# A fused attention and fp8 layer: the quantisation and bias of a head, in two halves, one behind each unit

## The reference

```python
xn = _layernorm(x)
# attention: 16 heads of 16 features over all 4096 tokens, softmax in float32
scores = einsum('bhqd,bhkd->bhqk', q, k);  ctx = einsum('bhqk,bhkd->bhqd', softmax(scores), v)
attn = ctx @ out_w.T + out_b
# ffn: both operands rounded to fp8 (e4m3), one scale for all of a tensor
x_fp8 = clip(xn * scale, -448, 448).astype(float8_e4m3fn)
ffn = (x_fp8 @ w_fp8.T * (x_scale * w_scale) + bias).astype(bfloat16)
```

## Time and profile before

| | us |
|---|---|
| median of three runs | 1858.34 (1856.72 to 1859.45) |
| the profiled execution | 1859.34 |
| its span, first to last instruction | 1857.5 |
| ACT busy | 1732.1 (93%) |
| PE busy | 1639.1 (88%) |
| DVE busy | 1606.8 (87%) |
| mean granted TensorE clock | 0.995 |

### The profile page before, as it was taken

How to read it: one execution, slowest core, us unless ns; L and a number is a source line. 1 busy time by engine, 2 the same in 40 slices (tenths; PEclk the granted TensorE clock), 3 DMA queues, 4 the chain that set the end, 5 groups by cost and what they waited for, 6 DMA issues and landing times.

```text
span 1857.5 us, 74891 instructions
## 1 busy us (share of the span) xinstructions
PE 1639.1 (88%) x33482; PEld 563.5 (30%) x33482; DVE 1606.8 (87%) x1831; ACT 1732.1 (93%) x1898; POOL 44.9 (2%) x57
## 2 busy tenths in 40 slices
PE   6889998998998889999988888888888888888888
PEld 4522322222222222222322222222222222222226
DVE  8689989899898989989888898888898988888895
ACT  2299999999999999999999999999999999999990
POOL 0000000000000000000000000000000000000003
PEclk9999999999999999999999999999999999999999
DMA  6401111101111111011110101101010001001014
GB/s 200 146 23 41 36 33 43 30 20 30 41 35 34 43 31 30 19 42 36 35 33 19 35 12 30 24 20 29 22 32 13 14 19 24 19 16 27 16 35 135
DMA packets 130169, 70.62 MB, mean 38 GB/s; under 512 B 79216, under 2 KB 120432, under 8 KB 129840
## 3 DMA queue, kind: packets, MB, share of 16 engines
q1 hardware_dynamic: 127920, 64.38, 13.1%
q10 hardware_dynamic: 1920, 1.39, 0.3%
HBM read 43.39 MB, written 17.83 MB: 33 GB/s over the span
## 4 chain that ended last, share of the span: by engine, by line
ACT 43%; issue 26%; PE 17%; DVE 10%; SPq 1%; DMA 1%; POOL 1%; ACTq 0%; DVEq 0%; POOLq 0%
ACT probs L851 43%; PE banks L1559 8%; PE banks L1505 5%; DVE bits L1203 2%; PE banks L1527 2%; DVE d_probs L1221 1%; DVE horner L1210 1%; DVE horner L1216 1%; DVE powers L1213 1%; PE banks L1409 1%; PE banks L1399 1%; DVE ctx_out L1181 1%; DVE powers L1207 1%; DVE o_sb L1180 1%; SPq L561 1%
## 5 line engine op out<-in xcount | busy, mean ns | idle before, releaser
L851 ACT ACTIVATE probs<-banks 128x1024 f32<-128x1024 f32 x1856 | 1709.1, 1140 | 18.4 <-issue 12.5
L1559 PE MATMUL banks<-probs,v_st 64*32 64x512 f32 x14848 | 970.1, 590 | 1.9 <-DVEq L1185 1.1
L1505 PE MATMUL banks<-q_st,k_st 50*32 50x512 f16 x16384 | 772.5, 381 | 185.2 <-ACT probs L851 166.6
L1505 PEld LDWEIGHTS banks<-q_st,k_st 50*32 50x32 f16 x16384 | 230.3, 89 | 1099.5 <-ACT probs L851 949.6
L1203 DVE TENSOR_SCALAR bits<-banks 128x1024 int32<-128x1024 f32 x192 | 235.0, 1224 | 86.9 <-PE banks L1505 81.6
L1559 PEld LDWEIGHTS banks<-probs,v_st 64*32 64x32 f32 x14848 | 264.9, 106 | 62.1 <-DVEq L1185 6.4
L1213 DVE SCALAR_TENSOR_TENSOR powers<-powers,horner 128x1024 f32<-128x1024 int32 x192 | 235.7, 1227 | 6.6
L1210 DVE SCALAR_TENSOR_TENSOR horner<-powers 128x1024 f32<-128x1024 int32 x192 | 235.5, 1227 | 6.6
L1216 DVE SCALAR_TENSOR_TENSOR horner<-powers,horner 128x1024 f32<-128x1024 f32 x192 | 235.2, 1225 | 6.6
L1221 DVE SCALAR_TENSOR_TENSOR d_probs<-horner,bits 128x1024 int32<-128x1024 f32 x192 | 235.1, 1225 | 6.6
L1207 DVE TENSOR_SCALAR powers<-bits 128x1024 int32<-128x1024 int32 x192 | 133.2, 694 | 6.6
(11 more groups left out here) (105 smaller groups left out, 426.5 us busy)
## 6 DMA issues: line engine op xcount, KB each, us to landing
late_x<-xnT_copy SPq DMA_DIRECT2D x32, 256.0 KB, 3.2
k_st<-k_parts SPq DMA_DIRECT2D x102, 64.0 KB, 2.3
q_st<-q_parts SPq DMA_DIRECT2D x198, 32.0 KB, 1.9
k_st<-k_parts SPq DMA_DIRECT2D x102, 60.0 KB, 2.2
q_st<-neg_row SPq DMA_DIRECT2D x264, 1.0 KB, 1.7
xnT_copy<-probs SPq DMA_DIRECT2D x8, 512.0 KB, 3.0
w_f<-xnT_copy SPq DMA_DIRECT2D x16, 256.0 KB, 2.9
xn_all<-ctx_out SPq DMA_DIRECT2D x128, 32.0 KB, 2.2
```

What stands on the lines that cost most here:

```text
L851: act.activation(probs[:, at:at + WIDE * CHUNK].rearrange("p (t c) -> p t c", t=WIDE), banks[:, bank:bank + WIDE, :], ACT.Exp, bias=EXP_SHIFT,
L1505: last = pe.matmul(banks[cols, bank + g, :], k_st[rows, keys], blocks[rows, j], start=True, stop=True, tile_position=(g * GROUP, t * VCOLS))
L1559: last = pe.matmul(banks[VCOLS * qb:VCOLS * (qb + 1), 6 + half, :], v_st[keys, kt, :], src[keys, g * CHUNK:(g + 1) * CHUNK], start=at == 0 ...
```

## The change

`quantise_part` is called behind each unit and does half of the work: 256 of the 512 columns of `xq`, and one of the two token tiles of `x_all`. The wait for the load (`xq_in`) stands in the call of unit 0. `xq_used` counts two per head, and the waits on it follow. The place of the load in SP's queue is the same.

```diff
-                        sp.wait_ge(xq_used, h + 1)
+                        sp.wait_ge(xq_used, h * UNITS + 1)
...
-                y, c, r = (t[:, :] for t in qt)
+                y, c, r = (t[:, 0:dst.shape[-1]] for t in qt)
...
-                def quantise_part(h):
+                def quantise_part(h, u):
 
-                    if h == 0:
+                    if h == 0 and u == 0:
                         for i in range(4):
                             dve.wait_ge(parts_saved[i], SAVED_0 + 32 * (NCH // 2))
-                    if h == HEADS * 3 // 4:
+                    if h == HEADS * 3 // 4 and u == 0:
                         for i in range(LATE_BUFS):
                             dve.wait_ge(late_saved[i], 16 * PARTS * LATE // LATE_BUFS)
-                    dve.wait_ge(xq_in, h * 16 + 16)
-                    dve.wait_ge(c.d_ready, block_at(h + 1, 0, 0))
-                    qn[0] = 0
+                    if u == 0:
+                        dve.wait_ge(xq_in, h * 16 + 16)
+                    dve.wait_ge(c.d_ready, block_at(h, u + 1, 0))
+                    qn[0] = u * QUANT_STEPS
...
-                        dve.wait_ge(quant_chain, h * QUANT_STEPS + qn[0])
-                    quantise(x8T[:, :, :].rearrange("p k s -> p (k s)")[:, span(h * CHUNK, CHUNK)], xq,
-                             fscale[:, 0, 2:3], qstep).then_inc(xq_used, 1)
-                    two = x_all[:, span(h * 2, 2), :]
-                    qstep(dve.tensor_tensor(two, two, bo_sb[:, :, :], ALU.add))
+                        dve.wait_ge(quant_chain, h * UNITS * QUANT_STEPS + qn[0])
+                    half = CHUNK // UNITS
+                    quantise(x8T[:, :, :].rearrange("p k s -> p (k s)")[:, span(h * CHUNK + u * half, half)],
+                             xq[:, u * half:(u + 1) * half], fscale[:, 0, 2:3], qstep).then_inc(xq_used, 1)
+                    one = x_all[:, span(h * 2 + u, 1), :]
+                    qstep(dve.tensor_tensor(one, one, bo_sb[:, u:u + 1, :], ALU.add))
...
-                    if u:
-                        quantise_part(h)
+                    quantise_part(h, u)
                     take_sums(h, u, lk + MAX_LINKS)
...
-            pe.wait_ge(xq_used, HEADS + 1)
+            pe.wait_ge(xq_used, HEADS * UNITS + 1)
```

## The result

| | before | after |
|---|---|---|
| median | 1858.89 us | 1985.62 us (1984.12 to 1987.98) |
| ratio | | 1.0685, 95% interval 1.0666 to 1.0703 |
| profiled execution | 1859.34 | 1984.12 |
| span | 1857.5 | 1982.2 |

The kernel is 126.7 us slower.

What follows compares the result with a forecast made beforehand. ACT's exponentials were taken to bound the attention. Lateness, half and slack gave 109.4 us; with clock 18 and 3, less 1.1, 129.3 on the profiled 1859.34: 1988.6, adjusted to the runs' median and stated as 1987 us, range 1950 to 2013.

Steps and rivals of the forecast that it cites:

- Part 4: PE's clock halving after stands: 2.0 us at each of nine boundaries (18), 3 us in all at the other seven.
- The bound: Through the attention ACT sets the pace, busy 53.60 of 53.80 us in a unit; what stops it lengthens the end.
- Part 1: End of unit 0, each head: the load of xq lands after the old start of the sums, 74.6 us in all.
- Part 2: Half a quantisation between the load's landing and the sums, 2.4 us in each of 16 heads: 38.4 us (27 to 55).
- Part 3: PE's place in hand in heads 8 to 15 takes off 0.45 us each: 3.6 us (0 to 7.4).
- The rule of the Trainium skill: A transfer wait in every tile throttles the clock each time; all 16 boundaries would pay, 28.5 us.
- Part 5: Gain after the last unit from a shorter last quantisation: -1.1 us (0 to -1.2); nothing gained behind the odd units.
- The clock that holds: Rival: same waits at the boundaries but PE's clock stays up, only 108.3 us added: 1966.6; chance 0.19.
- Given back: Rival: ACT runs closer behind a stall and 30 us come back, with the clock holding: about 1937; chance 0.10.
- The load early enough: Rival: the load lands early enough for the half to vanish in DVE's idle time in even units: 1857.3; chance 0.03.

Runs made afterwards that it cites:

- the wait alone: Kernel before, plus a DVE wait for the load of xq behind unit 0; whole quantisation stays behind unit 1: 1934.25 us, ratio 1.0413.
- the early load: Changed kernel with the load of xq issued in the middle of unit 0 from head 1 on: 1865.23 us, ratio 1.0046.
- both halves behind unit 1: Changed kernel with both halves of the quantisation behind unit 1, no wait in unit 0, load as before: 1864.30 us, ratio 1.0039.
- PE kept busy: Changed kernel with PE computing the scores of place 6 again, 11 to 64 times, in odd units while it stood: 1968.37 us, ratio 1.0595.
- the load first in the queue: Changed kernel with the load of xq ahead of saves, late loads and queries at unit 0's end, from head 1 on: 1898.81 us, ratio 1.0222.

## Why the prediction was right

Forecast 1987, measured 1985.62. The mechanism is the one that was forecast, but the closeness is in part luck: two errors in Part 4 cancel, and the sum of 129.3 us stands against 124.7 of span, of which 1.29 were gained ahead of the attention. By its own steps:

- **The bound.** Right. ACT sets the pace and has nothing to give: of 124.7 us of span, 124.8 are ACT's idle time at line 851.
- **Part 1, the lateness of the load.** Right, and shown by the wait alone and by the early load. The terms were 74.6 and the wait alone makes the sums 71.2 later. Head 8 is the one term that is off by more than 1 us: DVE waited 15.34 us there, not the nearly 18 that the prediction named, and the sums were 14.7 later, not 17.1. The load was issued 12.6 us behind the unit's first exponential, against 14.8 before. Why that queue ran 2.2 us faster wasn't tried; with the same order of its entries it was 12.8 with the wait alone, 13.6 with both halves behind unit 1 and 14.6 with PE kept busy. In head 14 the load took 3.9 us to land, and the sums came 4.0 later in place of 3.1.
- **Part 2, the half.** Right: 2.30 us from its first instruction to the sums in all 16, where 2.4 was taken with the start in it. The fixed part of 0.16 us of an instruction gave 0.43 us for 256 columns; measured are 0.426 (line 904). The price of 1.04 ns for a column doesn't hold for lines 901 to 903: 0.48 and twice 0.43 us at 512 columns became 0.35 and twice 0.29, 0.52 ns for a column, with 0.22 and twice 0.16 fixed. The sum took only the fixed part from there and halved the rest, so it is hardly touched. Parts 1 and 2 together: 113.0 expected, the sums came 109.7 later.
- **Part 3, the slack.** Right in kind. It is about 0.34 us a boundary in the later heads, not 0.45, and five of the first eight heads have 0.23, where I had 0. I had read both edges off weight loads. In the earlier trace rows it is the weight load that waited until 259.92; PE's matmuls of the sum ran on, and the scores followed at 260.26 without a wait. In the earlier trace rows the 0.40 is the weight load's too; the matmuls stood for 0.10.
- **Part 4, the clock.** The total was right and the split was not. With 0.23 and 0.34 of slack put back, heads 0 to 7 lost 0.4 to 1.4 us each beyond the delay, about 0.9 in the mean, and not 2.0; heads 9 to 15 lost 1.5 to 2.4 each, 2.0 in the mean, 14.2 in all, where I had 3. The total is about 23 with head 8 (when the 1.27 of unit 17 is put back), against 21; that the two errors cancel is luck. The rows tell why, though no run took it apart. At unit 3 the clock had fallen early in the long stand, and 4.0 of the low stretch's 10.1 us were left when PE started at 275.33; the slow sum lay beside the D block's first instruction (1.23 us at 275.37), for which PE had to wait anyway. At unit 21 the clock fell 1.6 us before PE started again, 5.1 us were left, and the slow sum (1.96) lay bare ahead of the scores of place 7. Over all boundaries two things go with the loss beyond the delay. One is how much of the low stretch was left when PE started: 0.2 us were lost with 2.9 left (unit 5), 0.55 with 4.0 (unit 3), 0.93 with 5.0 (unit 7). The other is the kind of unit: in the later ones 1.17 were lost with 3.1 left (unit 23), 1.71 with 4.2 (unit 29) and 2.01 with 5.1 (unit 25). The length of the stand isn't among them: 8.1 us in unit 5, 3.2 in unit 25. That the loss beyond the delay is the clock's is shown: with PE kept busy, 17 us go. How it splits between the heads is read from the rows alone.
- **The rule of the Trainium skill** ("TensorE: Matmul & The Clock Gate", "HAM oscillation — how this bites in real kernels"), that a wait in every tile throttles every tile, agrees with the trace: each of the 16 boundaries came with a stretch at 0.50. The sum that I gave by it, 28.5, was further off than my 21, because my prices were wrong.
- **Part 5.** Right where it can be seen: PE starts the output's first matmuls 1.24 us behind the last exponential, not 2.17, without the stand of 1.03. That the time ends earlier by it isn't shown. The tail from the last exponential on is 1.15 us shorter in the profile, but over the profiles of all nine kernels it lies between 46.9 and 50.8 us; the shortest is that of the wait alone, which keeps the whole quantisation at the end. The halved work behind the odd units gained nothing; the idle time ahead of the sums of unit 1 rose from 0.20 to 1.66. The wait of PE for keys in unit 17 (1.27 us), which is in the profile of the kernel before alone, was no part of the sum.
- **The rivals.** The clock that holds would have given 1966.6, and when it was held, 1968.4 were measured. Given back: fell, with even units equal within 0.01 us but for one. The load early enough: it wasn't so here, but made so, it gave no change.

## What to carry to other kernels

When a step is moved ahead on an in-order engine, look at when its data is issued and not only at whether the engine has time. Here the work fitted into the idle time, and the load that it needed was issued only behind PE's last scores of the unit and behind the transfers queued ahead of it. Here the wait was paid for by everything queued behind it, nearly one to one, since ACT had only 0.23 to 0.34 us in hand, and then a second time in TensorE's clock. Move the load first, measure, and then move the work.

## What was not expected of the hardware

Work that is thrown away can shorten a kernel. 408 extra groups of eight matmuls, in time in which PE stood, took the granted clock of the profiled execution from 0.960 to 0.991 and 17 us off (1985.62 to 1968.37; the ratio to before from 1.0685 to 1.0595). And the length of a stand alone didn't tell whether the clock fell. In the kernel with the wait alone PE stood 1.28 us ahead of its first sum in unit 21 and 1.34 in unit 29. The first came with a low stretch and a loss of 1.36 beyond the delay, the second with neither. Stands of 0.6 to 0.7 us in units 23, 25 and 27 came with none; with the load first in the queue, one of 0.76 in unit 3 came with a stretch at 0.50, and the unit lost 0.50 beyond the delay.
